# Spreading a slot's softmax denominators by one DMA instead of two, and loading staged weights by one, in a fused transformer block

## What is computed

```python
def _attention(xq, xkv, wq, wk, wv, wo, bo):
    q = (xq @ wq).reshape(B, S, N_HEADS, D_HEAD)
    k = (xkv @ wk).reshape(B, T, N_HEADS, D_HEAD)
    v = (xkv @ wv).reshape(B, T, N_HEADS, D_HEAD)
    attn = jnp.einsum('bihd,bjhd->bhij', q, k) * D_HEAD ** (-0.5)
    attn = jax.nn.softmax(attn, axis=-1)
    out = jnp.einsum('bhij,bjhd->bihd', attn, v).reshape(B, S, D_ATTN)
    return out @ wo + bo
h = _layernorm(x, ln1_g, ln1_b)
x = _attention(h, h, sa_wq, sa_wk, sa_wv, sa_wo, sa_bo) + x
h = _layernorm(x, ln2_g, ln2_b)
x = _attention(h, cond_emb, ca_wq, ca_wk, ca_wv, ca_wo, ca_bo) + x
h = _layernorm(x, ln3_g, ln3_b)
p = h @ ff_w1 + ff_b1
a, gate = (p[..., :D_FF], p[..., D_FF:])
x = a * jax.nn.gelu(gate, approximate=False) @ ff_w2 + ff_b2 + x
```

## Time and profile before

| | |
|---|---|
| median of 3 runs | 1717.55 us (1717.55 to 1719.23) |
| the profiled execution | 1720.14 us |
| its span in the trace | 1718.3 us |
| PE busy | 1702.5 us, 99% |
| DVE busy | 1467.4 us, 85% |
| ACT busy | 1186.3 us, 69% |
| POOL busy | 1087.9 us, 63% |
| granted clock of TensorE, mean | 0.999 |
| DMA issues of `spread_den` | 512, 64 KB each |
| DMA issues of the staged loads | 30 |

### The profile page before, as it was taken

The page is one execution under the profiler, slowest core; times in us unless marked ns, Lnnn a source line. Parts: engine busy times, 40 slices in busy tenths (PEclk is TensorE's granted clock), DMA queues, the critical chain, the costliest instruction groups (busy, mean ns, idle before and its releaser), DMA issues.

```text
span 1718.3 us, 42977 instructions
## 1 busy us (share of the span) xinstructions
PE 1702.5 (99%) x13628; PEld 1663.1 (97%) x13628; DVE 1467.4 (85%) x3184; ACT 1186.3 (69%) x3245; POOL 1087.9 (63%) x1812
## 2 busy tenths in 40 slices
PE   8999999999999999999999999999999999999999
PEld 8999999999999999999999999999999998888888
DVE  7888988888888888889999999999999997666665
ACT  6777777777777777777778878777777775222222
POOL 6777777766666666687778877777777665122211
PEclk9999999999999999999999999999999999999999
DMA  7777777676656666677777787776666662212110
GB/s 208 186 184 179 185 183 178 171 179 164 155 152 153 153 154 167 158 172 186 186 188 192 193 192 179 184 180 168 167 167 168 163 172 55 74 50 64 66 44 25
DMA packets 286641, 263.99 MB, mean 154 GB/s; under 512 B 102225, under 2 KB 246737, under 8 KB 286417
## 3 DMA queue, kind: packets, MB, share of 16 engines
q1 hardware_dynamic: 232624, 248.12, 57.1%
q10 hardware_dynamic: 53792, 13.12, 3.7%
HBM read 70.40 MB, written 24.90 MB: 55 GB/s over the span
## 4 chain that ended last, share of the span: by engine, by line
PE 90%; DVE 2%; SPq 2%; DMA 2%; POOL 2%; issue 1%; ACT 1%; ACTq 0%; POOLq 0%; DVEq 0%
PE QKB L341 19%; PE PVB L400 13%; PE PTB L355 12%; PE WOP L380 10%; PE VB L316 9%; PE S L303 6%; PE S L302 6%; PE PTB L920 5%; PE S L920 5%; PE QKB L936 3%; PE VB L936 3%; DMA RX<-QKS 1%; SPq L433 1%; SPq L435 1%; ACT PT L507 0%
## 5 line engine op out<-in xcount | busy, mean ns | idle before, releaser
L507 ACT ACTIVATE PT<-S,NM 128x256 f32<-128x256 f32 x1024 | 472.1, 474 | 186.0 <-DVE NM L613 185.6
L595 DVE TENSOR_TENSOR PL<-PTB,PH 128x512 fp32r<-128x512 f32 x512 | 349.4, 683 | 81.5 <-ACT PH L526 77.4
L811 POOL TENSOR_TENSOR ON<-ON,RB 128x256 f32<-128x256 f32 x256 | 188.9, 738 | 278.4 <-DVE ON L633 264.7
L613 DVE TENSOR_REDUCE NM<-S 128x2 f32<-128x512 f32 x512 | 325.9, 677 | 0.0
L526 ACT ACTIVATE PH<-PTB 128x1024 fp32r<-128x1024 f32 x256 | 263.4, 1029 | 90.3 <-PE PTB L355 87.3
L355 PE MATMUL PTB<-IDN,PT 128*128 128x128 f32 x2048 | 266.1, 273 | 0.1
L302 PE MATMUL S<-RX 128*128 128x256 f32 x1012 | 253.9, 283 | 0.2
L303 PE MATMUL S<-RX 128*128 128x256 f32 x1012 | 253.7, 283 | 0.0
L355 PEld LDWEIGHTS PTB<-IDN,PT 128*128 128x128 f32 x2048 | 229.5, 140 | 1.2 <-DVE PL L595 1.1
L380 PE MATMUL WOP<-WO,OT 128*128 128x256 f32 x1536 | 226.3, 283 | 2.3 <-POOL OT L816 2.3
L633 DVE TENSOR_TENSOR ON<-PVB,ON 64x256 f32<-64x256 f32 x512 | 213.1, 416 | 3.5
(11 more groups left out here) (142 smaller groups left out, 3142.4 us busy)
## 6 DMA issues: line engine op xcount, KB each, us to landing
RX<-QKS SPq DMA_DIRECT2D x506, 192.0 KB, 2.9
RX<-QKS SPq DMA_DIRECT2D x506, 128.0 KB, 2.8
RB<-denominators SPq DMA_DIRECT2D x512, 64.0 KB, 2.6
out_dram<-XR SPq DMA_DIRECT2D x32, 256.0 KB, 2.8
rows<-XN SPq DMA_DIRECT2D x24, 256.0 KB, 2.5
rows<-HF SPq DMA_DIRECT2D x23, 256.0 KB, 2.3
XR<-in_x_dram SPq DMA_DIRECT2D x16, 256.0 KB, 3.1
denominators<-RDT SPq DMA_DIRECT2D x256, 16.0 KB
```

Source lines behind the costliest of these rows:

```text
L507: last = e.activation(PT[:, c % 2, j * S:(j + 1) * S], S1[:, i, qt * S:(qt + 1) * S], ACT.Exp, bias=NM[:, j:j + 1], accum_out=DEN[:, c % 2 ...
L595: e.tensor_tensor(PL[:, cols], PTB[:, i, :], PH[:, s % 2, cols].bitcast(F32), ALU.subtract).then_inc(a.dve_pl, 1)
L613: e.tensor_reduce(NM[:, i * TT:(i + 1) * TT], S1[:, i, :].rearrange("p (t s) -> p t s", t=TT), AX.X, ALU.max, negate=True).then_inc(a.dve_ ...
```

## The change

The denominators of a slot are spread by one DMA: the source is two rows of 256 words, each repeated 64 times, the destination all 128 partitions. The staged matrices come by one DMA of 128 partitions each, except the two of which 64 rows are put on both halves, which keep two. The counts that are waited for follow (16 for each spread, and `staged(load)` for the loads). GpSimd splits load 1 in slots 5 to 8 instead of 4 to 7, and load 9 in slots 131 to 134 instead of 130 to 133.

```diff
+        def staged(load):
+
+            return 16 * (load + sum(load >= n for n in (2 + 3, 2 + 5)))
+
         def pool_split_wo(e, n, load, p):
 
             if load:
-                e.wait_ge(d_wst, 32 * load)
+                e.wait_ge(d_wst, staged(load))
...
-            if HALF <= c < PAIRS:
-                pool_split_wo(e, 0, 1, c)
+            if HALF < c <= PAIRS:
+                pool_split_wo(e, 0, 1, c - 1)
...
-            if SLOTS + 1 < c <= SLOTS + 1 + HALF:
-                pool_split_wo(e, 1, 3 + NCH, HALF + c - SLOTS - 2)
+            if SLOTS + 2 < c <= SLOTS + 2 + HALF:
+                pool_split_wo(e, 1, 3 + NCH, HALF + c - SLOTS - 3)
...
-                e.wait_ge(d_rb[s % 2], 32 * (s // 2 + 1))
+                e.wait_ge(d_rb[s % 2], 16 * (s // 2 + 1))
...
-            def stage(src, dst=STG[:, :]):
-
-                h = P // 2
-                for part, rows in ((slice(0, h), src[0]), (slice(h, P), src[1])):
-                    e.dma_start(dst[part], rows).then_inc(d_wst, 16)
+            def stage(rows, part=slice(0, P)):
+
+                e.dma_start(STG[part, :], rows).then_inc(d_wst, 16)
...
-                v = w.rearrange("(g p) n -> p g n", p=P)
-                stage((v[0:P // 2], v[P // 2:P]), STG[:, :].rearrange("p (g n) -> p g n", n=D))
+                e.dma_start(STG[:, :].rearrange("p (g n) -> p g n", n=D),
+                            w.rearrange("(g p) n -> p g n", p=P)).then_inc(d_wst, 16)
...
-                    e.wait_ge(d_rb[s % 2], 32 * ((s - 4) // 2 + 1))
+                    e.wait_ge(d_rb[s % 2], 16 * ((s - 4) // 2 + 1))
...
-                for i in range(2):
-                    e.dma_start(RB[OWN[i], s % 2, :],
-                                DS[s % 4, TT * i:TT * (i + 1), :].rearrange("t p -> (t p)").partition_broadcast(P // 2)) \
-                        .then_inc(d_rb[s % 2], 16)
+                e.dma_start(RB[:, s % 2, :], DS[s % 4, 0:2 * TT, :].rearrange("(i t) p -> i (t p)", i=2).unsqueeze(1)
+                            .to_broadcast([2, P // 2, S])).then_inc(d_rb[s % 2], 16)
...
-                if n % 2 == 0:
-                    stage((w[0:P // 2, :], w[P // 2:P, :]))
-                elif n == 1:
-                    stage((w[P:P + P // 2, :], w[P + P // 2:2 * P, :]))
+                if n % 2 == 0 or n == 1:
+                    stage(w[k * P:(k + 1) * P, :])
                 else:
-                    stage((w[P:DC, :], w[P:DC, :]))
+                    stage(w[P:DC, :], slice(0, P // 2))
+                    stage(w[P:DC, :], slice(P // 2, P))
...
-                    stage((w[0:P // 2, :], w[P // 2:P, :]))
+                    stage(w)
```

## The result

The changed kernel takes 1985.88 us (median of 4 runs, 1981.54 to 1989.6) against 1718.18 us: a ratio of 1.1558, 95% interval 1.1543 to 1.1573. That is 268 us more; 1903 us was forecast, in a range of 1735 to 2080.

A forecast was written before the change was run, and what follows sets the result against it. TensorE was taken to bound the kernel, busy 1702.5 of 1718.3 us; the change makes two DMA engines the limit. 1717.6 + 188 (spread) - 3 (later splits) = 1903 us, range 1735 to 2080.

The forecast's parts named there:

- The layout: In the one-transfer spread: 2 entries outermost in the source put it on 2 DMA engines, 64 packets of 1 KB each.
- Rival (a): The one-transfer spread still uses all 16 engines and costs nothing; 3 to 6 us gained, 1713 us; chance 10%.
- The packet time: For the spread's 1 KB packets: 48 ns each, so 3.0 us per slot on each of two engines.
- The load: Work per slot on the spread's two DMA engines: 5.7 to 6.8 us, against TensorE's 5.66 and 5.42.
- the loop: In SP's queue, a save lands behind the previous spread and the next spread waits for it: 5.6 us spread to spread.
- I take 6.3: Slot period in both attentions, chosen just over the middle of 5.7 and 6.8 us: +188 us over 250 slots.
- Late next: What the slower spread delays: the ring copies, first for ScalarE's L469, then for the scores, in most slots.
- Rival (b): Two engines, but nearly hidden as slots share slack: about +35 us in cross attention, 1720 to 1755 us; chance 9%.
- Rival (c): Spread loop (5.6 us) and ring copies (1.9) add to 7.5 us a slot: +488 us, 2200 us; chance 11%.
- Part 2: Staged matrices loaded by one transfer each: 13 issues of about 0.6 us leave SP, costed at 0.
- Part 3: GpSimd's splits of loads 1 and 9 a slot later, ending L741's waits for the loads: -3 us.

The follow-up runs named there:

- the run by columns: The changed kernel with the spread cut into two transfers by columns, each to all 128 partitions, 128 words per row: 1953.35 us, ratio 1.1362.
- half the words: The changed kernel spreading only the first 128 of 256 words of each row, still by one transfer: 1719.08 us, ratio 1.0000.

## Why the prediction was right, and what it had too small

**The layout** was right: two engines for a source with 2 entries outermost, read off a transfer with 4. 224736 packets, the 11.7% of 16 engines, and the run by columns show it. The rule that the Trainium skill states for it in "DMA: Bandwidth & Descriptors", section "Why a DMA increments its semaphore by 16 and not by 1", holds here for 2 and for 4; that it is the lowest-numbered engines, no trace here shows. The advice that the Trainium skill gives in "Rules for kernel authors" of the same page, one transfer in place of two to disjoint halves, holds for the staged matrices (2.5 us gained, against nothing costed) and fails for the spread, where one transfer has another outermost dimension. Rival (a) is out.

**The packet time**, 48 ns from the earlier trace rows, was measured at 46.

**The load** of the two engines, 5.7 to 6.8 us by the ring copies' two speeds, came out at 6.10 a slot where SP no longer waits for the save. How much of the copies ran at either speed was not separated.

**The step that was mis-sized is the loop.** "5.6 us from spread to spread" took the spread's shortest landing (2.4) with 60 more packets and the save behind it. By the save's semaphore it lands 5.65 us after its issue (median; 2.21 before), and its issue is 0.67 after the spread's (median; 305.31 and 305.99 above), so the loop takes over 6.3 us, and the median from spread to spread is 6.46. Two errors were in the 5.2 us from a spread's issue to its landing, and they partly cancel. With nothing in front it is too much: the last three spreads, after the last ring copies, land in 4.4 to 4.5 us. With the ring copies it is too little: the median is 6.04, for the copies of the slot before stand in front of the spread on the two engines. Of all other spreads there is none whose copies have landed when it is issued; they land 2.2 us later (median), and L435's copies 4.2 us after their issue where it was 2.8 before. That this is the whole of the missing 0.7 us fits the numbers and was not tried by itself. I let load and latency take each other's slack; in fact the load lengthens the loop. "I take 6.3" should have been 6.63, and 250 slots times 0.33 are the 83 us by which the forecast was low. The 6.3 was chosen between two bounds and not added up from parts, so that it came this near is in part luck.

**Late next** were the ring copies, at L469 first and then at L302, as forecast; at L469 in most slots (222 times), at L302 in fewer than half (PE 84 times, PEld 121), where "most" was written for both. PE busy was forecast under 95% and is 92%.

**Rival (b)**, hidden by averaging: not at this load, but at 1.2 us less, as half the words show, all of it. **Rival (c)**, the full sum of 7.5 us, needed the copies to wait for the loop's end; SP issues them 1.35 us into it (306.66 after 305.31).

**Part 2** was costed at 0 and gains 2.5 us by itself. **Part 3** was costed at -3 and gains 2.4. In the changed kernel both drown. One term of part 2 was also taken from the kernel before and doesn't hold in the changed one: the landing of the staged loads, 4.2 to 4.7 us, is 6.9 to 8.8 us there for those of 512 KB (medians; 4.1 to 5.2 with the spread in two), and GpSimd waits for them for 21.2 us in all.

## What to carry to other kernels

Before two transfers are merged into one, look at the outermost dimension on both sides: a broadcast "two rows, each 64 times" has 2 there, and that, not the 128 partitions it reaches, set the number of DMA engines: the staged loads reach 128 partitions by one transfer too, and each still reports 16 completions. Two engines of 16 can be the bound at a mean DMA share of 59% (from 30 to 1700 us); the share is a mean, and the number of completion packets or a stretch with one transfer alone tells how many engines work. And a small transfer that others wait for belongs ahead of a large one in its queue. It took hardly less time to land for it here (5.46 us for 5.65), but there was 1 us more between it and the issue that waits for it, and that order alone was worth 131 us.

## What the runs showed that I had not expected

TensorE's clock fell in the middle of the attentions, ten times. Before, its mean granted share is 0.999, after it 0.990. Busy time by stretches around one such place of the changed kernel:

```profile
290.00:296.00 6.00, 5.80 (x47) 5.51 (x46) 4.75 (x11) 2.31 (x5) 2.96 (x5) 1.00 0.80 203
296.00:300.00 4.00, 2.08 (x17) 1.90 (x16) 0.87 (x4) 2.65 (x10) 2.92 (x5) 0.97 0.60 180
300.00:304.00 4.00, 4.00 (x24) 4.00 (x24) 3.77 (x7) 3.32 (x11) 1.13 (x2) 0.61 0.76 169
304.00:308.00 4.00, 3.18 (x27) 2.98 (x27) 0.89 (x4) 0.54 (x3) 2.90 (x5) 1.00 0.20 55
```

PE was busy for 2.08 of 4 us; then the granted clock was 0.61 over the next 4 us, part of it at 1.2 GHz instead of 2.4, with 24 matmuls in 4.00 us of busy time where 3.18 us held 27 right after. In this place TensorE had been idle for 1.92 us behind ScalarE. Another place shows a ring copy before it: L302 starts at 415.04 after 1.76 us of waiting for the copy, and the twelve matmuls of L341 behind it take 2.91 us, where twelve took 1.70 one slot earlier. A stall of the copies can thus cost once more afterwards. Over the span it is small: 0.010 x 1987 less 0.001 x 1718 is some 18 us of clock time, at most 7% of the loss, and how much of it was on the path is not shown. It is also part of why PE's busy time grew from 1702.5 to 1832.7 us for the same 13628 matmuls; busy time is no measure of work here.
